# Second attention: the low half of the turned outputs, from VectorE to GpSimd

## What is computed

```python
h = _layernorm(x, gamma, beta)                       # x: 16 x 56 x 128
Q = (h @ Wq).reshape(B, NQ, 16, 64)
K = (context @ Wk).reshape(B, NC, 16, 64)            # context: 16 x 1500 x 96
V = (context @ Wv).reshape(B, NC, 16, 64)
attn = jax.nn.softmax(jnp.einsum('bihd,bjhd->bhij', Q, K), axis=-1) * scale
vals = jnp.einsum('bhij,bjhd->bihd', attn, V).reshape(B, NQ, 1024)
return x + vals @ Wo + bo
```

## Time and profile before

| | us |
|---|---|
| median of 3 runs (lowest, highest) | 1037.78 (1037.33, 1039.84) |
| the profiled execution | 1036.11 |
| its span, first to last instruction | 1034.0 |
| PE busy in it | 964.8 |
| DVE, ACT, POOL busy | 735.0, 575.0, 444.8 |

### The profile page before, as it was taken

One profiled execution on the slowest core, in us unless ns is written; L12 is line 12 of the kernel. 1 busy time (PEld: TensorE's weight loads), 2 busy tenths in 40 slices (PEclk: granted clock), 3 DMA queues, 4 the chain that ended last, 5 costly groups with the idle time before them and its releaser, 6 DMA issues.

```text
span 1034.0 us, 28022 instructions
## 1 busy us (share of the span) xinstructions
PE 964.8 (93%) x11883; PEld 697.4 (67%) x11883; DVE 735.0 (71%) x1329; ACT 575.0 (56%) x1117; POOL 444.8 (43%) x326
## 2 busy tenths in 40 slices
PE   5967999999999999896799999999999999999997
PEld 3643677777677776654377777777777777777776
DVE  6756888888888886477667666777666777667652
ACT  3622777777777777665644444444444444444452
POOL 6524222332243213044655545555455554555542
PEclk9965999999999999899899999999999999999998
DMA  3606999899989942200213212132121232123210
GB/s 130 164 25 142 208 178 204 172 198 184 177 201 203 181 126 51 70 2 1 70 37 78 76 42 78 41 80 79 52 65 44 78 78 59 58 49 73 55 22 4
DMA packets 120928, 99.16 MB, mean 96 GB/s; under 512 B 78931, under 2 KB 105653, under 8 KB 120805
## 3 DMA queue, kind: packets, MB, share of 16 engines
q1 hardware_dynamic: 120804, 97.39, 42.1%
HBM read 51.10 MB, written 22.18 MB: 71 GB/s over the span
## 4 chain that ended last, share of the span: by engine, by line
PE 43%; DVE 4%; ACT 1%; DMA 1%; issue 1%; POOL 0%; SPq 0%; ACTq 0%
PE PS L1644 6%; PE PS L1645 6%; PE PS L1646 6%; PE PS L1110 6%; PE PS L1662 5%; PE PS L1664 5%; PE PS L1663 5%; DVE Ol L1785 3%; PE PS L1685 2%; ACT Oh L1753 1%; DMA Qh<-QK 1%; DVE m L1119 1%; PE PS L1698 0%; POOL Pl L1627 0%; PE PS L1674 0%
## 5 line engine op out<-in xcount | busy, mean ns | idle before, releaser
L1741 ACT ACTIVATE P<-PS 125x448 f32<-125x448 f32 x384 | 208.1, 544 | 272.2 <-PE PS L1646 270.3
L1627 POOL TENSOR_TENSOR Pl<-P 125x896 f16<-125x896 f32 x128 | 230.6, 1806 | 236.8 <-ACT P L1741 236.6
L1119 DVE TENSOR_REDUCE m<-PS 128x1 f32<-128x500 f32 x336 | 217.2, 673 | 101.5 <-PE PS L1110 99.5
L1015 DVE TENSOR_REDUCE m_part<-PS 128x1 f32<-128x500 f32 x336 | 214.3, 676 | 39.4 <-PE PS L913 36.7
L989 ACT ACTIVATE Pb<-PS 125x448 f32<-125x448 f32 x384 | 187.4, 547 | 48.5 <-PE PS L882 48.1
L1662 PE MATMUL PS<-cNh,P 125*128 125x97 f16 x1344 | 197.9, 208 | 0.1
L1664 PE MATMUL PS<-cNh,Pl 125*128 125x97 f16 x1344 | 197.4, 207 | 0.0
L1663 PE MATMUL PS<-cNl,P 125*128 125x96 f16 x1344 | 196.8, 206 | 0.0
L1663 PEld LDWEIGHTS PS<-cNl,P 125*128 125x128 bf16 x1344 | 131.8, 98 | 27.4
L1662 PEld LDWEIGHTS PS<-cNh,P 125*128 125x128 bf16 x1344 | 131.2, 98 | 17.4 <-issue 3.2
L1644 PE MATMUL PS<-Qh,cTh 110*125 110x448 f16 x384 | 138.8, 362 | 1.3 <-DVE Qh L1826 1.3
(11 more groups left out here) (214 smaller groups left out, 1505.0 us busy)
## 6 DMA issues: line engine op xcount, KB each, us to landing
Kst<-k_halves SPq DMA_DIRECT2D x144, 125.0 KB, 2.9
k_halves<-KH SPq DMA_DIRECT2D x16, 750.0 KB, 4.4
cx<-in_ctx SPq DMA_DIRECT2D x32, 281.2 KB
d_cx<-in_ctx SPq DMA_DIRECT2D x16, 562.5 KB
c_halves<-cHi SPq DMA_DIRECT2D x16, 288.0 KB, 3.4
c_halves<-cLo SPq DMA_DIRECT2D x16, 288.0 KB, 8.3
cTh<-c_halves SPq DMA_DIRECT2D x16, 288.0 KB, 3.0
cTl<-c_halves SPq DMA_DIRECT2D x16, 288.0 KB, 3.9
```

The costliest lines, as they stand in the source:

```text
L1015: nc.vector.tensor_reduce(m_part[:, t, part:part + 1], PS[:, 6 + k % 2, 0:SP], AX.X, ALU.max).then_inc(s_reduced, 1)
L1119: nc.vector.tensor_reduce(m21[:, t, part:part + 1], PS[:, S1[k % 2], 0:SP], AX.X, ALU.max).then_inc(n_red, 1)
L1627: nc.gpsimd.tensor_tensor(Pl[:, c % NP], P1[:, c % NP], high, ALU.subtract).then_inc(n_low_p, 1)
L1741: nc.scalar.activation(P1[:, c % NP, half * HALF:(half + 1) * HALF], PS[0:KC, u % 3, 0:HALF], ACT.Exp).then_inc(n_exp, 1)
```

## The change

The low half `Ol` of the batch before's output is made by GpSimd and no longer by VectorE. In GpSimd's queue it stands at c = 2, that is behind its `Pl` of chunks 0 and 1 and ahead of that of chunk 3 (chunk 2 is VectorE's). `finish_batch`, which overwrites `On`, now waits for `Ol` of the batch before where it waited for `Oh`. Operands, sizes and the waits of `output_low` itself are the same.

```diff
+                def output_low(n):
+
+                    pool.wait_ge(n_oh, n + 1)
+                    wait_for(pool, n_ot, n * 32)
+                    nc.gpsimd.tensor_tensor(Ol[:, :, 0:DC], On[:], Oh[:, :, 0:DC], ALU.subtract).then_inc(n_ol, 1)
+
                 def body(i, par):
                     b = i * 2 + par
                     for c in range(NC):
@@
                             nc.gpsimd.tensor_tensor(Pl[:, c % NP], P1[:, c % NP], high, ALU.subtract).then_inc(n_low_p, 1)
+                        if inside(i, par, 0) and inside(i, par, -1) and c == 2:
+                            output_low(b - 1)
                         if inside(i, par, 1) and c == 4:
@@
                     dve.wait_ge(n_r, n * 2 + 2)
-                    wait_for(dve, n_oh, n)
+                    wait_for(dve, n_ol, n)
@@
-                def output_low(n):
-
-                    dve.wait_ge(n_oh, n + 1)
-                    wait_for(dve, n_ot, n * 32)
-                    nc.vector.tensor_tensor(Ol[:, :, 0:DC], On[:], Oh[:, :, 0:DC], ALU.subtract).then_inc(n_ol, 1)
@@
                     for c in range(NC + LAG):
                         pieces = list(BESIDE1[c]) if has_b and has_1 else []
-                        if has_b and has_old and c == 2:
-                            output_low(b - 1)
```

## The result

The changed kernel takes 1022.42 us (median of 3 runs, 1022.30 to 1022.70) against 1037.78 before; the ratio is 0.9847, 95% interval [0.9825, 0.987]. That is 15.4 us less. The profiled execution took 1022.30 us with a span of 1020.2.

The account below looks back on a forecast made before the run. PE bounds the kernel, shortened only by losing waits: 11 x 0.89 + 3 x 0.61 = 11.6 us in step 3, so 1037.78 - 11.6 = 1026.2 us; range 1024.0 to 1031.0.

Parts of the forecast that it names:

- How the numbers follow: Closing part: gain 9.9 to 13.4 us plus run scatter gives 1024.0 to 1030.0, extended to 1031.0; forecast chance 0.86.
- `Ol` leaves VectorE: Second attention, step 3: 2.70 in place of 3.59 us in eleven batches, 0.61 less in three; 11.6 us in all.
- The upper bound of 13.4: Whole kernel: gain of 13.4 us if the 1.8 us of waits for `Qh` don't come again.
- The lower bound taken from batch 0: Steps 3 and 4: batch 0's 0.12 us excess over steps 6 and 7, times 14, leaves a 9.9 us gain.
- some 31: Profile after: DVE has 15 instructions fewer and is some 31 us less busy.
- What `Ol` cost: VectorE, step 2: of `Ol`'s 2.08 us, 1.37 is waiting out GpSimd's instruction; it then needs 0.71.
- GpSimd gets `Ol`: GpSimd, steps 2 and 3: `Ol` takes 1.43 us, bounds 1.03 and 2.30, in a gap of 2.1.
- The cover over VectorE's `Pl`: `Pl` of chunk 2, step 3: loses nothing while GpSimd's `Ol` takes under 1.62 us; cover 0.19 us at 1.43.
- The warning of the Trainium skill: GpSimd and VectorE share an SBUF port, so the move might bring nothing: 1037.8; rival "nothing", chance 0.04.
- Reductions beside GpSimd: VectorE reductions L1119 do not wait GpSimd out: all 336 keep one duration, 0.68 us alone.
- The transfers: `Ol` ready 0.7 us later, landing at 783.8, worst 785.6, against batch 8's projection at 785.6: hidden.
- Batch 15: Last batch: GpSimd's `Pl` of chunks 3 and 4 pushed about 0.9 us, 0.7 us over; nothing either way.

Follow-up runs that it names:

- Behind the reductions: Kernel before, with VectorE keeping `Ol` but behind the reductions of step 2, not ahead of them: 1024.71 us, ratio 0.9876; again 1027.53 us, ratio 0.9896.
- The larger variants: Changed kernel with a second GpSimd instruction ahead of `Ol`, into an unread buffer: 192 columns 1030.01 us, ratio 0.9927; 672 columns 1042.73 us, ratio 1.0051.

## Why the prediction failed, point by point

**The step that failed** is the one in "How the numbers follow" that turned 11.6 us into a range: "the runs scatter from 0.5 below to 2.1 above their median". That took three runs of one kernel for the whole scatter, and left out a fourth time that stood beside them, the profiled execution at 1036.11, 1.67 below the median. The lower bound was its own 13.4 us of gain and 0.5 of scatter. What the runs showed in its place: of the first comparison's 15.36 us, 3.66 lay outside the second attention, where no instruction was changed. The base of the subtraction, 1037.78, was one set's value (other sets of the same program had medians of 1036.55, 1037.06, 1037.18, 1037.45 and 1039.82), and so was the time after (1022.42, then 1026.56 and 1026.14). Single executions of the kernel before lie between 1032.89 and 1042.47. The first comparison caught the changed kernel at 514.5 us for the part ahead, near the low end of twelve profiles, 513.8 to 522.3. Three runs within 2.5 us of each other did not show this scatter; the 1036.11 was a hint of it, though even with 1.67 in place of 0.5 the range would have ended at 1022.7, above 1022.42. So the forecast's size and mechanism were right, and that the first time fell outside the range was bad luck; that the medians over all executions come out 12.3 us apart, near 11.7, is partly luck too, with medians of single sets 3.3 us apart for one program.

**`Ol` leaves VectorE: right.** In eleven batches step 3 is 2.71 us in place of 3.59; in the three others 2.71 in place of 3.31, 3.44 and 3.31. The sum of the changes in steps 3 and 4 over the 14 batches is 11.7 us (11.5 in step 3, 0.2 in step 4); forecast 11.6. The upper bound of 13.4 did not come true either: the waits for `Qh` came again, three times. The lower bound taken from batch 0, whose step 4 is 2.65 us, did not come true for the others: they have 2.52. One sign was off: VectorE is busy 24.3 us less (735.0 to 710.7) and not some 31. That figure was the sum of the records of `Ol` (30.7 us), which overlap with their neighbours, and the reductions, more of them now alone, are busy 2.9 us longer.

**What `Ol` cost: right.** 0.71 us of its own and a wait for GpSimd. In all 15 batches it ended 0.71 to 0.72 us behind GpSimd's instruction. Behind the reductions it takes 0.85 us. That the 0.14 between them is an overhead which lay in the wait before is my reading; `Pl` has the same distance, 1.08 us alone and 0.95 behind GpSimd.

**GpSimd gets `Ol`: right.** 1.46 us against 1.43 from the line between two sizes. The cover over VectorE's `Pl` was put at 0.19 us; `Ol` ended at 740.00 and could have ended at 740.08 + 1.08 - 0.95 = 740.21. The warning of the Trainium skill (Perfetto Trace Analysis, Optimizing Scalar/DVE Operations) that a move between these two engines might bring nothing did not come true here: in that stretch VectorE had no instruction that waits for GpSimd. The larger variants show when it would.

**Reductions beside GpSimd: right.** They keep 0.68 us while GpSimd makes `Ol` (739.49 in the time line of DVE).

**The transfers: right.** In batch 8 the transfer of `Ol` was issued at 771.11 + 1.30 = 772.41, with 4.6 us to the landing at worst in this profile; the projection started at 777.39.

**Batch 15: right**, with the wait the other way about. GpSimd's `Ol` started inside VectorE's `Pl` there and took 2.31 us in place of 1.46:

```profile
987.17 2.31 POOL L1625 TENSOR_TENSOR Ol<-On,Oh 128x672 f16<-128x672 f32 x1
```

```profile
986.52 1.65 DVE L1839 TENSOR_TENSOR Pl<-P 125x896 f16<-125x896 f32 x1 [3.19 <-ACT P L1749]
```

The steps of that batch are the same to 0.01 us.

**What stays open** is what decides in the part ahead whether PE drops to the lower clock in a given execution, and why the same program, measured beside itself, differed by 0.31% [0.15%, 0.47%] in one set and not measurably in another.

## What to carry to other kernels

Price a change by the interval in the trace that it touches, and check it by that interval; against the total it drowns, here differences of 0.5 us between variants against 2.2 us of spread per execution (one standard deviation over 76). And look at the granted clock of the interval first: a step without any gap took 3.07 us or 2.16. When a short instruction of VectorE is long in the record, look at what GpSimd is in: its end plus a fixed time says that it waited. And before handing work to another engine, try it one or two places later in its own queue: here that alone gave 11.2 of the 11.7 us in the two steps concerned (10.2 to 10.5 over the whole second attention, with the slower clock at its start).

## What the runs showed of the hardware that was not expected

The forecast took the two engines' mutual wait from one distance, 0.71 us for 672 columns, and scaled it; 896 columns then measured 0.95 us behind GpSimd's end in the two kernels with more work for GpSimd, 672/0.71 = 947 and 896/0.95 = 943 columns a us. GpSimd's own rate for these types: 96 columns 0.37 us, 192 0.55, 672 1.46, which is 1.9 ns a column and 0.19 us of fixed time. And the spread between executions of one program, 1032.89 to 1042.47 us: three profiles of the changed kernel differ by 6.2 us in the part ahead and by 0.3 in the second attention. The second attention begins at the lower clock in all twelve profiles; matmuls of L1645 take 0.58 us there in the kernel before and 0.35 once the clock has risen.
